# A decoder layer with routed experts on one core: experts in rounded three-part products, weights split during attention, a ring of three experts

## The reference, cut to what matters

```python
base_y = _silu_mul(x @ base_gate_up) @ base_down          # 256 -> 2*512, silu(gate)*up, 512 -> 256
probs = softmax(x @ gate_w); w, idx = top_k(probs, 2); w = w / w.sum()
for e in range(8):
    y = _silu_mul(x @ expert_gate_up[e]) @ expert_down[e]
    out = out + comb[:, e:e + 1] * y                      # comb holds w at idx, else 0
x = layernorm(x + out + base_y)
```

## Time and profile before

| | |
|---|---|
| median of three runs | 735.15 us |
| profiled execution, its span | 725.34 us, 723.5 us |
| TensorE matmul busy | 660.0 us (91%) |
| TensorE weight load busy | 391.4 us (54%) |
| VectorE, ScalarE, POOL busy | 383.3, 309.7, 135.3 us |
| instructions in all | 10370 |
| DMA traffic | 40.01 MB, mean 55 GB/s |
| mean granted TensorE clock | 0.978 |

### The profile page before, as it was taken

One profiled execution on the slowest core, in us unless ns is written; L12 is line 12 of the kernel. 1 busy time (PEld: TensorE's weight loads), 2 busy tenths in 40 slices (PEclk: granted clock), 3 DMA queues, 4 the chain that ended last, 5 costly groups with the idle time before them and its releaser, 6 DMA issues. The chain is left out here.

```text
span 723.5 us, 10370 instructions
## 1 busy us (share of the span) xinstructions
PE 660.0 (91%) x3039; PEld 391.4 (54%) x3067; DVE 383.3 (53%) x884; ACT 309.7 (43%) x661; POOL 135.3 (19%) x155
## 2 busy tenths in 40 slices
PE   2778999999989999998679899999999999999991
PEld 2445555555545554543266566666666666666660
DVE  3568788898877888887625621111221211111286
ACT  2346666666656666665542112222222222222115
POOL 2011111111011111111000200233333333332100
PEclk9999999999999999999998999999999999999996
DMA  6100000000000000000049800011111111111343
GB/s 181 29 23 23 18 6 22 23 24 24 23 24 8 14 22 15 15 15 2 0 156 388 304 7 0 30 50 39 41 50 39 43 38 44 40 43 38 104 129 116
DMA packets 33073, 40.01 MB, mean 55 GB/s; under 512 B 5404, under 2 KB 28447, under 8 KB 33024
## 3 DMA queue, kind: packets, MB, share of 16 engines
q1 hardware_dynamic: 29280, 30.10, 12.8%
q0 software_dynamic: 3744, 9.31, 4.1%
HBM read 31.01 MB, written 9.31 MB: 56 GB/s over the span
## 5 line engine op out<-in xcount | busy, mean ns | idle before, releaser
L1299 PE MATMUL inner<-up,sortedT 128*128 x312 | 146.7, 592 | 0.0
L1162 DVE TENSOR_TENSOR hidden<-silu,inner 128x512 f32<-128x512 f32 x55 | 37.8, 686 | 170.8 <-PE inner L1299 170.1
L1039 ACT ACTIVATE silu<-inner 128x512 f32<-128x512 f32 x55 | 32.8, 597 | 191.6 <-PE inner L1299 191.6
L438 ACT ACTIVATE prob<-scores 128x1024 f32<-128x1024 f32 x96 | 98.3, 1026 | 11.5 <-PE scores L785 7.4
L565 DVE TENSOR_REDUCE max_c<-scores 128x8 f32<-128x1024 f32 x64 | 78.0, 1219 | 6.9 <-PE scores L848 5.8
L1299 PEld LDWEIGHTS inner<-up,sortedT 128*128 128x128 f32 x312 | 56.2, 190 | 39.4 <-issue 37.3
L1322 PE MATMUL y<-down,hT 128*128 x312 | 73.8, 379 | 0.0
L1015 POOL DMA_INDIRECT chosen_y<-y_rows,to_row x39 | 39.6, 1015 | 179.4 <-DVE y_rows L1173 175.5
L872 PE MATMUL sums<-prob,v_c 128*32 128x512 f32 x256 | 63.7, 621 | 0.0
L1299 PE MATMUL inner<-base_up,router_xT 128*128 128x512 f32 x128 | 61.4, 606 | 0.0
L1322 PEld LDWEIGHTS y<-down,hT 128*128 128x128 f32 x312 | 56.4, 190 | 7.0 <-issue 1.0
(11 more groups left out here) (187 smaller groups left out, 1052.2 us busy)
## 6 DMA issues: line engine op xcount, KB each, us to landing
up<-in_exp_gu SPq DMA_DIRECT2D x8, 1024.0 KB, 13.3
down<-in_exp_down SPq DMA_DIRECT2D x8, 512.0 KB, 12.2
up<-chosen_y SPq DMA_DIRECT2D x8, 512.0 KB, 8.3
xT_in<-in_xT SPq DMA_DIRECT2D x16, 128.0 KB, 2.2
x_in<-in_x SPq DMA_DIRECT2D x16, 128.0 KB, 2.2
x<-stream SPq DMA_DIRECT2D x1, 2048.0 KB, 10.0
ctxT_in<-in_ctxT SPq DMA_DIRECT2D x16, 96.0 KB, 2.3
out<-stream SPq DMA_DIRECT2D x2, 768.0 KB, 3.7
```

The costliest lines, as they stand in the source:

```text
L438: act.activation(prob[:, m, :], scores[:, n, :], ACT.Exp, scale=scale).then_inc(sem[exped], 1)
L1039: act.activation(silu[q % 2][:], inner[:, q % 2, 0, :], ACT.Silu).then_inc(sem["silu_set"], 1)
L1162: dve.tensor_tensor(hidden[q % 2][:], silu[q % 2][:], inner[:, q % 2, 1, :], ALU.mult).then_inc(sem["hidden_set"], 1)
L1299: mm = pe.matmul(inner[:, q % 2, h, :], tokens(q, k), w, start=(k == 0), stop=(k == 1))
```

## The change

Five things change.

1. **Products.** The experts' products and the base network's first one become three-part products of float32r values. A sorted tile has 6 products of 512 columns per half (`split_products`' order, in `half`) and 12 of 256 columns in `outer`. The base network's second product stays float32.
2. **Weights.** The eight experts' weights come as 16 halves. During attention each step loads one half (SP, `load_w`), POOL splits it (`w_high`, three `w_low`), and SP stores both parts to HBM (`store_w`). In `experts` a ring of three experts in SBUF is filled from there; expert e + 3 is loaded when y of expert e's last tile is complete. A tile now reads two registers: its ring slot, and the number of experts that must be ready.
3. **Base network.** Four tiles form a group. Its first product has the weights stationary and 512 tokens moving, so that silu(gate)*up comes out transposed, in four chunks, and nothing is turned. Two groups run ahead of the sorted tiles and two behind.
4. **Turning.** x2 is transposed tile by tile in attention (`x2_turn` on TensorE, `x2_read` on ScalarE, a new user of `misc`), and stored tile by tile.
5. **Loops.** Attention is written out, without the loop.

```diff
-            for s in range(FIRST_STEP, LOOP_FROM):
-                step(s)
-            with eng.Fori(0, LOOP_STEPS // UNROLL) as i:
...
+            for s in range(FIRST_STEP, LAST_STEP + 1):
                 step(s)
...
+    ("x2_turn", 0, -2),                                     # PE_ORDER, last; ("x2_read", 0, -2) last of ACT_ORDER
 POOL_ORDER = [
-    ("s_split", 0, 4), ("c_keys", 0, 1), ("x_bias", 0, 2),
+    ("s_split", 0, 4), ("w_high", 0, 2), ("c_keys", 0, 1), ("w_low", 0, 2), ("w_low", 1, 2),
+    ("x_bias", 0, 2), ("w_low", 2, 2), ("base_split", 0, 2),
 ]
 SP_ORDER = [
     ("load_xT", 0, 4), ("load_ctx", 0, 2), ("load_base", 0, 2), ("load_x", 0, 2),
+    ("store_w", 0, 1), ("load_w", 0, 3), ("store_x2", 0, -2),
 ]
...
+            def w_high(seq, unit):
+                p = seq.odd
+                wait_loaded(pool, w_loaded, seq)
+                if seq.off >= 2:
+                    wait_loaded(pool, split_stored, seq.back(2))
+                pool.tensor_copy(halves[p][:, 0, :], raw_w[p][:]).then_inc(sem["w_high"], 1)
+
+            def w_low(seq, third):
+                p, n = seq.odd, HALF // 3                   # HALF = 1536
+                wait(pool, sem["w_high"], seq)
+                pool.tensor_tensor(halves[p][:, 1, n * third:n * third + n], raw_w[p][:, n * third:n * third + n],
+                                   f32(halves[p][:, 0, n * third:n * third + n]), ALU.subtract).then_inc(sem["w_low"], 1)
...
+            for e in range(RING, EXPERTS):
+                done = sp.value_load(free_after[0:1, e - RING:e - RING + 1], min_val=FIRST_OUTS, max_val=FIRST_OUTS + SORTED)
+                sp.wait_ge(sem["y_full"], done)
+                load(e)
+                ready(e)
...
+            def base_half(g, c, h):
+                u, at = use_of("base", g, c), INNER * h + P * c
+                into = inner[:, u % 2, h, :]
+                free_inner(u, h)
...
+                for k in range(2):
+                    pe.matmul(into, base_hi[:, k, at:at + P], xg_hi[g % 2][:, k, :], start=(k == 0), stop=False)
+                    pe.matmul(into, base_lo[:, k, at:at + P], xg_hi[g % 2][:, k, :], start=False, stop=False)
...
+                for k in range(2):
+                    mm = pe.matmul(into, base_hi[:, k, at:at + P], xg_lo[g % 2][:, k, :], start=False, stop=(k == 1))
...
+            def half(j, h):
...
+                if h == 0:
+                    pe.wait_ge(sem["turned_hi"], j + 1)
+                    if j == 0:
+                        pe.wait_ge(sem["tile_set"], 1)
+                    slot_of[j] = pe.value_load(tile_slot[0:1, j:j + 1], min_val=0, max_val=RING - 1)
+                    needed = pe.value_load(tile_ready[0:1, j:j + 1], min_val=1, max_val=EXPERTS)
+                free_inner(u, h)
+                if h == 0:
+                    pe.wait_ge(sem["weights_ready"], needed)
...
+            def outer(j):
...
+                pe.wait_ge(sem["hT_hi"], j + 1)
+                reach(pe, sem["y_read"], o)
+                for c in range(CHUNKS):
+                    pe.matmul(into, hT[:, j % 2, 0, P * c:P * c + P], w(0, c), start=(c == 0), stop=False)
+                    pe.matmul(into, hT[:, j % 2, 0, P * c:P * c + P], w(1, c), start=False, stop=False)
+                pe.wait_ge(sem["hT_lo"], j + 1)
+                for c in range(CHUNKS):
+                    mm = pe.matmul(into, hT[:, j % 2, 1, P * c:P * c + P], w(0, c), start=False, stop=(c == CHUNKS - 1))
...
+            base_chunk(0, 0)
+            base_chunk(0, 1)
+            rank_tokens()
+            base_chunk(0, 2)
+            base_chunk(0, 3)
+            base_chunk(1, 0)
+            base_outer(0)
+            find_rows()
+            for c in range(1, CHUNKS):
+                base_chunk(1, c)
+            turn_rows(0)
+            turn_rows(1)
+            base_outer(1)
+            half(0, 0)
+            half(0, 1)
...
+            for c in range(1, CHUNKS):
+                base_chunk(GROUPS_FIRST, c)
+            base_chunk(GROUPS_FIRST + 1, 0)
+            base_outer(GROUPS_FIRST)
+            for c in range(1, CHUNKS):
+                base_chunk(GROUPS_FIRST + 1, c)
+            base_outer(GROUPS_FIRST + 1)
```

The order of a sorted tile on TensorE stays that of the job above. VectorE gets two subtractions a tile, for the low parts of the turned hidden tile (512 columns, `turn`) and of the turned rows (256 columns, `turn_rows`), ahead of and behind the product of the next tile. Its order behind the sorted tiles is new:

```diff
+            for m in range(CHUNKS - 1):
+                for t in later[m]:                          # [0, 1], [2, 3], [4, 5]
+                    add_shares(t)
+                multiply(u + CHUNKS + m)                    # chunks 1 to 3 of the last group
+            for t in later[3]:                              # [6, 7]
+                add_shares(t)
+            for m in range(TILES):
+                take(first + TILES + m)
+                if m < 2:
+                    add_shares(8 + 2 * m)
+                    add_shares(9 + 2 * m)
+            variance(0)
+            add_shares(12)
+            newton(0)
+            for t in range(13, B):
+                add_shares(t)
```

More of the change, by code:

```diff
@@ L933, in experts @@
         lane_hot = sb("lane_hot", [P, PICKS, P], BF16)
+        hidden = [lane_hot[:, 8 * p:8 * p + 8, :].rearrange("p a b -> p (a b)").bitcast(F32) for p in range(2)]
         slot_hot = sb("slot_hot", [P, PICKS, SLOTS], BF16)
@@ L967, in reach, with f32, y_bank @@
                 eng.wait_ge(s, v)
-        def sorted_before(q):
-            return sum(kind == "sorted" for kind, _ in jobs[:q])
-        def base_before(q):
-            return sum(kind == "base" for kind, _ in jobs[:q])
+        def f32(ap):
+            return ap.bitcast(F32)
+        def y_bank(o):
+            kind, n = outs[o]
+            return hiddenT[:, 0:2, :].rearrange("p a b -> p (a b)") if kind == "base" and n % 2 else y[:, 0:D]
         block = scope.enter_context(nc.Block())
@@ L1221, in _ @@
             choose_second()
[L1222 to L1237 removed]
+            multiply(1)
@@ new lines, in _ @@
+            group_low(1)
+            multiply(2)
+            place_picks()
+            multiply(3)
+            hot_lanes()
+            multiply(4)
+            take(0)
+            take(1)
+            hot_slots()
+            take(2)
+            take(3)
+            multiply(5)
+            tile_experts()
+            multiply(6)
+            slot_rows()
+            multiply(7)
+            turn_rows(0)
+            turn_rows(1)
+            for o in range(TILES, FIRST_OUTS):
+                take(o)
@@ new lines, in _ @@
+            multiply(use_of("sorted", 0))
+            for j in range(SORTED):
+                if j:
+                    take(outs.index(("sorted", j - 1)))
+                if j == SORTED - 2:
+                    group_low(GROUPS_FIRST)
+                if j == SORTED - 1:
+                    group_low(GROUPS_FIRST + 1)
+                turn(j)
+                multiply(use_of("sorted", j) + 1)
+                if j + 2 < SORTED:
+                    turn_rows(j + 2)
+            take(outs.index(("sorted", SORTED - 1)))
@@ new lines, in _ @@
+            u = use_of("base", GROUPS_FIRST, 1)
+            for m in range(CHUNKS):
+                multiply(u + m)
+            first = FIRST_OUTS + SORTED
+            later = [[0, 1], [2, 3], [4, 5], [6, 7]]
+            for m in range(TILES):
+                take(first + m)
+            for m in range(CHUNKS - 1):
+                for t in later[m]:
+                    add_shares(t)
+                multiply(u + CHUNKS + m)
+            for t in later[3]:
+                add_shares(t)
```

427 lines of the change are left out of this document (268 added, 159 removed).

## The result

The changed kernel takes 765.14 us (median of four runs, 764.03 to 772.66), the kernel before in the same session 733.77: ratio 1.049, 95% interval [1.036, 1.063]. It is slower by 5%, where 717 us were forecast.

The account below looks back on a forecast made before the run. TensorE's product rate was taken to bound the second half; sorted tiles would idle 0.8 us each. First sorted tile at 431.2, plus 218.4 and tail 56.5, gave 706.1 us span, times 1.0135 after adding 1.84: 717 us, range 684 to 744.

Parts of the forecast that it names:

- 1.6 us for VectorE held up by POOL: Attention: VectorE loses 0.1 us a step to POOL's added work, 1.6 us in all.
- POOL takes VectorE's time in attention: Rival, attention: VectorE and POOL wait for each other; steps grow by 2 us, 32 us in all, timed 750; chance 0.13.
- Transposes of x2: Attention: two transposes a step and a change of weights add 0.3 us each step on TensorE, +4.8 us.
- Loop's edge: Attention: writing out the loop removes 3.4 us from the step across its edge.
- The copy of 1536 columns on POOL: Attention: one added POOL copy per step, 1.8 us at half the split's price, 3.8 at full; 1.8 taken.
- 1.3 us, then the logits, 9.05.: Start of the experts: after the last x2, transposes, copy and barrier take 1.3 us, then logits 9.05, ending at 384.2.
- my 4.4: First two groups: TensorE waits 4.4 us for gathered rows ahead of y.
- my 1.8: First two groups: a start at 1.2 GHz, as in the kernel before, costs 1.8 us.
- The reads are hidden: Rival, sorted tiles: sequencer work runs fully beside the array, a tile takes 4.8 us, timed 686; chance 0.24.
- If an expert's weights come late the cost is open: Sorted tiles: no cost set for late expert weights; expert e + 3 has some 50 us for 3.1 MB.
- my 20.4: Tail: 20.4 us from the first base product behind the sorted tiles until VectorE can begin with the shares.
- My 11: Tail: y of the last group begins about 11 us after VectorE can begin with the shares.

Follow-up runs that it names:

- Gated: The changed kernel with POOL's splits moved inside the attention step, behind the context keys and the bias; 727.0 us, ratio 0.996 to the kernel before.
- Warm: The changed kernel with the first two chunks of the base network ahead of the router's logits; 780.0 us, ratio 1.065 to the kernel before.
- reads_ahead: The changed kernel with both register reads of a sorted tile moved ahead of TensorE's wait for the hidden tile; 761.9 us, ratio 1.046.
- ahead5: The changed kernel with gathers issued five tiles ahead instead of three; 760.9 us, ratio 1.042 to the kernel before.
- dma_only: The changed kernel with all weight loads and stores in attention, but POOL splitting only the first two halves; 727.8 us, ratio 1.000.

## Why the prediction was wrong

**Attention, +36.3 us: the step that failed.** "Against no gain and no loss at best I put 1.6 us for VectorE held up by POOL, 0.1 a step." It was 2.8 us a step (23.26 against 20.47 without the splits), about 2.0 of standing and the rest the clock that fell in every other step. Gated against changed, 374.1 for 410.1, shows that the place of the splits is nearly all of it. The rival named it, "POOL takes VectorE's time in attention", with 32 us and 750 in time, and put the turning point at 1.1 us a step; it got 0.13. It did not have the clock either. I had looked at one pair only, the rows' parts. These were hardly touched (353 ns for 288). I had not listed VectorE's other lines beside the splits. The two Newton lines read two SBUF operands; the normalizations read one tensor in SBUF and write SBUF, and were held too. They stand right behind the context keys, where the order put the splits. A one-column instruction of 0.16 us seemed to have nothing to lose; it loses the length of what it waits for. The Trainium skill, page SBUF — State Buffer, section Who interferes with whom, says that a VectorE instruction with two SBUF inputs and a GpSimd one that reads SBUF exclude each other; the traces agree: 1660 and 1220 ns for 158.

**Its other terms held.** Transposes of x2: 20.47 - 20.25 = 0.22 a step, predicted 0.3. Loop's edge: 3.1 us, predicted 3.4. The copy of 1536 columns on POOL: 1.47 us, I took 1.8; splits of 512 1.28. Gated ends at 374.1 where 373.8 was forecast. That it is so close is in part luck: its two steps of 21.6 us beside the base network's split, 2.2 us together, were in no term, and the transposes (1.3 us less than forecast) and the 1.6 us for VectorE, which gated does not have, made up for them.

**Logits, +5.1.** "1.3 us, then the logits, 9.05." I carried over the 9.05 and removed the work that earned it: the 32 transposes in the earlier trace rows, right ahead of the logits. Behind them the clock was 1.00 for the first 5.0 us of the logits. Without them the logits run at 1.2 GHz throughout. Warm shows 8.91 us for them behind two chunks.

**First groups, +0.7.** 47.7 for 47.0. Gathered rows kept TensorE waiting 2.4 us and the low part of the first ones 1.0, for my 4.4, and the other waits were 1.0 for my 2.7. Against that, the half clock up to 430.68 cost 2.5 for my 1.8; a second stretch of it behind the wait for rows, 464.6 to 468.0, made the first y 1.4 us longer and was in no term; and a chunk took 2.8 us for my 2.7. The small error is a sum of larger ones.

**Sorted tiles, +12.3.** The tile was right (5.67 for 5.6), and for the reason given: reads_ahead makes it 4.87, which is the 4.78 of the array's work and 0.09 (a 512-column product takes 0.233 us for my 0.225). "The reads are hidden" was wrong as the kernel stood, and one edit makes it true. The step that failed is "If an expert's weights come late the cost is open": the weights came in time, and their loads delayed the gathers. That is 10.8 us by ahead5; its 219.9 us are 39 tiles of 5.64, and 1.5 us above the forecast is the rest.

**Tail, +1.7.** Shares began at 728.08, 24.1 us behind the first base product, for my 20.4: I had left out the last sorted tile's turn and y (1.8 us), which stand between the two halves. The last group's y began 10.1 us later. My 11 for this was an error of addition, since the three terms that I gave sum to 12.4. What followed took 24.0 us for my 25.1. A tile's shares take 1.37 us, as in the earlier trace rows.

**The scale.** I multiplied by 1.0135, the loop kernel's median over its profiled execution. The changed kernel's own factor is 765.14/764.03 = 1.0015. This put 8.5 us too much into the forecast and hid part of the error.

## What to carry to other kernels

Before work goes to POOL because it "has room", list VectorE's instructions in the stretch where it will stand, and mark those with two SBUF operands, however short, and the wide ones from SBUF to SBUF; put POOL's work beside VectorE's reads of PSUM. A register read is free where the sequencer waits anyway; behind the last product two of them cost 0.8 us a tile here. When a wait of some microseconds goes in or out, look at the clock behind it too. When work is removed, ask what it kept up, the clock or the cover of a wait; when two waits stand on one chain, measure the repairs together before either is dropped.

## What the runs showed that was not expected

- Cutting POOL's instructions into pieces does not let VectorE in reliably: a normalization of 0.41 us took 2.59 beside pieces of 0.43 us.
- A wide normalization with one tensor operand (128x256, 0.41 us) is held as well, up to 2.08 us (x) and 2.46 us (stream) in the changed kernel, 2.58 us (x) beside the base network's split in dma_only; an instruction of the same kind with one column is never held (0.20 to 0.22 us in all 64 cases).
- The clock can fall in the middle of dense-looking work: TensorE was busy 10.00 of 10.00 us in both stretches above, with the logits in both, and the clock fell from 1.00 to 0.50 at 387.4, 2.8 us into the logits.
- Repairs of 8.3 and 10.8 us in the sorted stage gave 41.3 together.
- Attention of the same code ended between 410.1 and 418.1 us in different kernels, with the clock at 0.50 for 28 to 48 us of it.
